# The last film of a four-layer sequence kernel: batch 0 normalized during the attention's last groups, turns and out pairs of the two batches interleaved, four stores

## What is computed

```
q = xn @ q_w + q_b;  k = xn @ k_w + k_b;  v = (xn @ v_w + v_b) * mask     # xn = layer_norm(x)
att = softmax(q k^T + mask term, over the keys)                            # 16 heads of 16 channels
y = att v                                                                  # 1024 x 256 for each batch
scale, shift = split(silu(emb) @ emb_w + emb_b)
h = layer_norm(y, sb_norm_w, sb_norm_b) * (1 + scale) + shift
return x + silu(h) @ out_w + out_b
```

## Time and profile before

| | us |
|---|---|
| median of three runs | 2120.67 |
| lowest and highest | 2118.75, 2123.79 |
| the profiled execution | 2122.75 |
| its span in the profile | 2121.0 |
| busy in the span: TensorE, VectorE, ScalarE, GpSimd | 1739.7, 1822.9, 1211.9, 1147.5 |
| mean granted TensorE clock, as a share of full speed | 0.889 |

### The profile page before, as it was taken

The page is one execution under the profiler, slowest core; times in us unless marked ns, Lnnn a source line. Parts: engine busy times, 40 slices in busy tenths (PEclk is TensorE's granted clock), DMA queues, the critical chain, the costliest instruction groups (busy, mean ns, idle before and its releaser), DMA issues.

```text
span 2121.0 us, 23810 instructions
## 1 busy us (share of the span) xinstructions
PE 1739.7 (82%) x8210; PEld 651.4 (31%) x8210; DVE 1822.9 (86%) x2159; ACT 1211.9 (57%) x2171; POOL 1147.5 (54%) x585
## 2 busy tenths in 40 slices
PE   5788879678797888678788888796897899999985
PEld 2222213132231323232322222232663333333323
DVE  4699999899999999999998999999547888888803
ACT  3766465645656666555565666543452266666672
POOL 2688877877888887789898787764000000000000
PEclk9898979869697899899997999887998799999998
DMA  6152522222223232322222232331061522220001
GB/s 198 56 160 79 95 71 75 66 61 71 75 70 98 79 95 80 87 70 72 91 81 88 74 100 73 108 90 46 1 121 39 83 33 32 32 32 2 2 2 40
DMA packets 95941, 149.83 MB, mean 71 GB/s; under 512 B 24291, under 2 KB 31651, under 8 KB 95412
## 3 DMA queue, kind: packets, MB, share of 16 engines
q1 hardware_dynamic: 95820, 148.31, 27.1%
HBM read 137.05 MB, written 10.62 MB: 70 GB/s over the span
## 4 chain that ended last, share of the span: by engine, by line
PE 40%; DVE 34%; issue 9%; POOL 8%; ACT 7%; DMA 2%; SPq 0%; DVEq 0%; ACTq 0%; POOLq 0%
DVE hbuf L2331 19%; DVE hbuf L2312 7%; PE psum L1721 6%; PE psum L731 6%; POOL hbuf L1421 6%; PE psum L697 5%; PE psum L717 4%; PE psum L612 3%; PE psum L1510 3%; DVE gain L1012 2%; PE psum L601 2%; PE psum L1673 1%; PE psum L1518 1%; PE psum L1537 1%; DMA cbuf<-scr_c 1%
## 5 line engine op out<-in xcount | busy, mean ns | idle before, releaser
L1421 POOL TENSOR_TENSOR hbuf<-hbuf,cbuf 128x1024 f32<-128x1024 f32 x384 | 901.8, 2358 | 272.9 <-DVE hbuf L2331 141.2
L2119 ACT ACTIVATE psum<-slots,cols 128x512 f32<-128x512 f32 x708 | 485.5, 689 | 392.0 <-DVE hbuf L2331 387.9
L1721 PE MATMUL psum<-hbuf,ident 64*64 64x512 f32 x3072 | 491.6, 715 | 172.8 <-POOL hbuf L1421 172.2
L2312 DVE TENSOR_TENSOR hbuf<-slots,psum 128x1024 f32<-128x1024 f32 x354 | 422.1, 1193 | 49.8 <-POOL slots L1338 30.3
L2331 DVE TENSOR_TENSOR_SCAN hbuf<-psum,hlast,hbuf 128x512 f32<-128x512 f32 x354 | 432.5, 1263 | 8.7 <-ACT psum L2119 8.7
L2331 DVE TENSOR_TENSOR_SCAN hbuf<-psum,hbuf 128x512 f32<-128x512 f32 x354 | 411.1, 1200 | 8.8 <-ACT psum L2119 8.8
L1012 DVE TENSOR_REDUCE gain<-psum 128x1 f32<-128x512 f32 x512 | 315.4, 680 | 59.2 <-PE psum L697 58.7
L563 POOL COPY wl<-hbuf 128x512 f32<-128x512 f32 x8 | 4.8, 613 | 429.1 <-PE psum L731 400.4
L697 PE MATMUL psum<-slots 99*128 99x512 bf16 x512 | 197.1, 400 | 23.9 <-DVE gain L1012 11.5
L717 PE MATMUL psum<-slots 102*128 102x512 bf16 x512 | 194.5, 388 | 6.5 <-ACT xn_flat L895 1.7
L1721 PEld LDWEIGHTS psum<-hbuf,ident 64*64 64x64 f32 x3072 | 91.0, 147 | 318.3 <-POOL hbuf L1421 255.4
(11 more groups left out here) (278 smaller groups left out, 2234.3 us busy)
## 6 DMA issues: line engine op xcount, KB each, us to landing
cbuf<-scr_c SPq DMA_DIRECT2D x384, 256.0 KB, 3.2
slots<-scr_qk SPq DMA_DIRECT2D x96, 128.0 KB
wl<-scr_diag SPq DMA_DIRECT2D x18, 256.0 KB, 4.7
scr_qk<-slots SPq DMA_DIRECT2D x8, 512.0 KB, 2.8
wl<-in_w SPq DMA_DIRECT2D x8, 496.0 KB, 4.9
wl<-in_ada_w SPq DMA_DIRECT2D x1, 3584.0 KB
xt<-in_x SPq DMA_DIRECT2D x2, 1024.0 KB, 12.5
wl<-in_w SPq DMA_DIRECT2D x2, 1024.0 KB, 7.0
```

Source lines behind the costliest of these rows:

```text
L1421: pool.tensor_tensor(hs, hs, cbuf[:, at % CRING:at % CRING + 1, :].to_broadcast([P, 2, TC]), ALU.mult).then_inc(weighed, 1)
L1721: last = pe.matmul(psum[side, bank, :], ident[rows_of, rows_of], hbuf[rows_of, at % RING, q, :], start=False, stop=n == NS - 1, skip_group ...
L2119: act.activation(decay_bank(at, q), dts[k % 2][:, e, :], ACT.Exp, scale=coefficient(WORK[k], e, n)).then_inc(decay, 1)
L2312: dve.tensor_tensor(hbuf[:, at % RING, :, :], ws[k % 2][:, 2 * p:2 * p + 2, :], psum[:, 2 + at % 2:3 + at % 2, :].to_broadcast([P, 2, TC]) ...
```

## The change

- VectorE measures and normalizes y3[0] in group 57 of the loop (MEASURE_Y3), behind that group's division; ScalarE's first `deviation()` stands behind the exps of group 58.
- The pieces of the last films are listed in another order (LAST_FILMS) and use banks 4 to 7. TensorE first makes sure that the maxima's banks have been read.
- Behind the last weighing TensorE turns batch 0 (token half 0 first: pieces 0, 2, 1, 3), then does turn_out of the last half job, then batch 0's out pairs 0 and 1 once the two silus of token half 0 are done, then batch 1's turns once y3[1] is normalized, then batch 0's pairs 2 and 3, then batch 1's four pairs, by token halves.
- ScalarE: silu table, batch 0's silus, exp table, `deviation()` for batch 1, silu table, batch 1's silus. The last load of the exp table is gone.
- VectorE: behind the last division it measures and normalizes y3[1], then adds all eight pairs.
- SP stores half a batch at a time, four DMAs of 512 KB, each as soon as its two pairs are added; `x_done` is gone.

```diff
+MEASURE_Y3 = JOBS * TT - TT + 1
...
-                  ("2hT", 1), ("2out", 1), ("3xT", 1), ("3q", 1), ("3k", 1), ("3v", 1),
-                  ("3hT", 0), ("3out", 0), ("3hT", 1), ("3out", 1)):
+                  ("2hT", 1), ("2out", 1), ("3xT", 1), ("3q", 1), ("3k", 1), ("3v", 1)):
     STAGES += [(_name, _b, i) for i in range(1 if _name == "2m" else 4)]
+BY_SIDE = (0, 2, 1, 3)
+LAST_FILMS = [("3hT", 0, i) for i in BY_SIDE] + [("3out", 0, i) for i in range(2)]
+LAST_FILMS += [("3hT", 1, i) for i in BY_SIDE] + [("3out", 0, i) for i in (2, 3)]
+LAST_FILMS += [("3out", 1, i) for i in range(4)]
+STAGES += LAST_FILMS
...
-            return psum[:, T[key] % 4, :]
+            return psum[:, T[key] % 4 + (4 if key in LAST_FILMS else 0), :]
...
+            def last_out(b, pairs):
+                to_tokens("3out", b, h3T[b], w3[:, 3], OB3, pairs)
...
             weigh(JOBS - 1, 1, TT // 2 - 1)
+            pe.wait_ge(maxed, JOBS * 2 * UNITS)
+            pe.wait_ge(max_read, JOBS)
+            pe.wait_ge(h_ready, 3)
+            to_wide("3hT", 0, y3[0], BY_SIDE)
             turn_out(2 * JOBS - 1)
-            pe.wait_ge(normalized, 2 * JOBS)
-            for b in range(BATCH):
-                film("3", 3 + b, b, y3[b], h3T[b], w3[:, 3], OB3)
+            after_act("3hT", 0, 2)
+            last_out(0, (0, 1))
+            pe.wait_ge(h_ready, 4)
+            to_wide("3hT", 1, y3[1], BY_SIDE)
+            after_act("3hT", 0, 3)
+            last_out(0, (2, 3))
+            for side in range(2):
+                after_act("3hT", 1, BY_SIDE[2 * side + 1])
+                last_out(1, (2 * side, 2 * side + 1))
...
+            def last_hidden(b):
+                for i in BY_SIDE:
+                    k, n = divmod(i, 2)
+                    act.activation(h3T[b][:, k, n * 512:n * 512 + 512], get("3hT", b, i), ACT.Silu,
+                                   scale=f_cols[:, 1, b, 0, k:k + 1], bias=f_cols[:, 1, b, 1, k:k + 1]).then_inc(t_act, 1)
...
-            for b in range(BATCH):
-                deviation()
-            for b in range(BATCH):
-                film(3, b, h3T[b])
+                if g == MEASURE_Y3 + 1:
+                    deviation()
+            act.preload_act_table_set("silu_and_others")
+            last_hidden(0)
+            act.preload_act_table_set("natural_log_exp_and_others")
+            deviation()
+            act.preload_act_table_set("silu_and_others")
+            last_hidden(1)
...
+                if g == MEASURE_Y3:
+                    dve.wait_ge(normalized, JOBS)
+                    measure(y3[0])
+                    normalize(y3[0], y3[0], h_ready)
             take_out(2 * JOBS - 1)
             divide_out(2 * JOBS - 1)
             dve.wait_ge(normalized, 2 * JOBS)
+            measure(y3[1])
+            normalize(y3[1], y3[1], h_ready)
             for b in range(BATCH):
-                measure(y3[b])
-                normalize(y3[b], y3[b], h_ready)
-            for b in range(BATCH):
-                add_out("3out", b, x_done)
+                add_out("3out", b, None)
...
             for b in range(BATCH):
-                sp.wait_ge(x_done, b + 1)
-                sp.dma_start(out[b].rearrange("(i p) d -> p i d", p=P), xt[:, b * TT:(b + 1) * TT, :]).then_inc(stored, 16)
-            sp.wait_ge(stored, 16 * BATCH)
+                for side in range(2):
+                    sp.wait_ge(t_dve, t_taken(("3out", b, 2 * side + 1)))
+                    at = b * TT + side * TB
+                    sp.dma_start(out[b, side * TC:side * TC + TC].rearrange("(i p) d -> p i d", p=P),
+                                 xt[:, at:at + TB, :]).then_inc(stored, 16)
+            sp.wait_ge(stored, 32 * BATCH)
```

More of the change, by code:

```diff
@@ L400, in build @@
         scanned, weighed, summed = sem("scanned"), sem("weighed"), sem("summed")
-        saved, y_free, x_done = sem("saved"), sem("y_free"), sem("x_done")
+        saved, y_free = sem("saved"), sem("y_free")
         ld_fcols, f_cols_ready, keep_ready = sem("ld_fcols"), sem("f_cols_ready"), sem("keep_ready")
@@ L587, in start, with to_wide @@
                 return stage_bank(key)
[L589 to L595, removed]
+            def to_wide(name, b, src, pieces=range(2 * KD)):
+                for i in pieces:
+                    ps, (k, n) = start(name, b, i), divmod(i, 2)
+                    for q in range(4):
+                        last = pe.transpose(ps[:, q * P:(q + 1) * P], src[:, n * 4 + q, k * P:(k + 1) * P], ident[:, :])
+                    last.then_inc(t_done, 1)
             def project(name, b, w, src, pieces=range(4)):
```

## The result

Seven executions of the changed kernel took 2105.09 us in the median (2097.49 to 2113.79), seven of the kernel before 2120.93 (2118.75 to 2125.02): a ratio of 0.9917, with a 95% interval of 0.9892 to 0.9941. The prediction was 2104.4. The profiled execution took 2110.42.

The account below looks back on a forecast made before the run. Engines waiting on each other in the last groups, then a serial tail, bound the kernel. TensorE's end 2100.55 + 0.11 + 0.69 + 3.39 = 2104.74 against 2121.0, 16.3 less; from median 2120.67 that gives 2104.4 us, range 2100.7 to 2110.0.

Parts of the forecast that it names:

- Term 1: Group 58 to 59: ScalarE's Ln and Exp for batch 0 add 0.54 us (bounds 0 and 1.2); VectorE's 6 us cost nothing.
- Term 2: Behind the last weighing: batch 0's turns ahead of turn_out(15) delay batch 1's measuring by 1.22 us (bounds 1.0 and 2.9).
- Term 3: Tail: batch 1's measuring starts at 2076.83 instead of 2081.65, its turns at 2083.59; all three table loads cost nothing.
- Term 4: TensorE from batch 1's turns: 1.91 us, six pairs 13.44, one low clock stretch 1.6 (bounds 0 and 4.3), ending at 2100.55.
- rival A': Tail: no fall of TensorE's clock, 1.6 us less, 2102.8 us; chance 0.15.
- Term 5: End of the kernel: 0.11 and 0.69 us for the last addition, then 3.39 for the store instead of 4.89.
- the prediction's other estimate: Last store, by the skill page's fixed 2.0 us: 3.5 us instead of 2.9, the end 0.6 later.
- Rival B: Tail: a second low stretch, from batch 0's turns through batch 1's next two pairs, 4.3 us instead of 1.6, 2107.1; chance 0.11.
- C: Tail: clock low to the end, all turns and six pairs, 13.7 us instead of 1.6, 2116.5; chance 0.04.
- D: Loop: VectorE comes late to group 57, so ScalarE stands up to 6.6 us for batch 0's normalizing, 2111; chance 0.02.
- E: Last five groups: the hole at group 59 brings the clock down, 22.8 us together, 2127, slower; chance 0.02.

Follow-up runs that it names:

- the better version: Changed kernel with batch 0's deviation behind group 58's fourth exp, turn_out between batch 0's turns, half of batch 1 normalized in the loop: 0.9899 of the kernel before.

## Why the prediction was right, point by point

- *Term 1, 0.54 for the deviation in the loop*: 0.41 by the period. VectorE had 5.35 us to spare before take_out, forecast 4.8. That nothing hides ScalarE's pair held for the place where the change puts it; behind the fourth exp it costs nothing.
- *Term 2, +1.22 for batch 0's turns ahead of turn_out*: 0.87 (3.06 against 2.19 from the copy's start to the measuring), under its lower bound of 1.0. I took the turns' 1.91 less the copy's 0.69; the turns start 0.13 before the copy, and the old turn also waited for the copy's hand-over.
- *Term 3, what falls off the chain*: from the measuring to the turns 6.73 us (2082.49 to 2089.22), forecast 6.76. The loads were hidden as said, with 1.83 us to spare for ScalarE, forecast 1.9.
- *Term 4, TensorE*: from the first turn of batch 1 to the last addition's start 15.45 us (2089.22 to 2104.67); the sum has 1.91 + 13.44 + 0.11 = 15.46 without the clock. The 1.6 us for a low stretch was not paid in the profiled execution, nor in the second one: both are rival A', to which I had given 0.15, and whose tail by the prediction's steps is 29.7. Where the stretch came, in the run with the deviation amid a group, it cost 2.7, because it held the turns and most of a pair, and I had priced it by a stretch that held pairs alone. One fall in four executions at 2.7 us is 0.7 on average, against the 1.6 of the sum. So this term was the one most in error.
- *Term 5, the store*: 3.34 from the last addition's end, forecast 3.39; four stores against two 1.6, forecast 1.5. The Trainium skill's advice to join transfers ("DMA: Bandwidth & Descriptors", "Rules for kernel authors") points the other way. For a store that ends the program the rows decide against it: 4.4, 2.9 and 2.1 us (medians) for 1024, 512 and 256 KB, by which about 1.4 is fixed and the rest goes by bytes, and only the last one's fixed part is on the path. For 512 KB that is 2.9, and not the 3.5 of the prediction's other estimate.
- *Rival B* (a low clock from batch 0's turns on) did not come: TensorE went through 20 turns in a row at the high clock. The prediction read the turns and first two pairs of the old tail as one low stretch. They were two: the clock was full from 2085.2 and fell anew in the wait of 4.38 us. Another window of the kernel before, beside the earlier trace rows:

```profile
2088.00:2089.00 1.00, 0.00 (x0) 0.00 (x0) 0.30 (x1) 1.00 (x3) 0.00 (x0) 0.79 0.00 0
```

  The Trainium skill's "TensorE: Matmul & The Clock Gate", Part 4, has transposes not counted as busy in the same way. The traces show both sides. A wait of 1.57 us behind turns was followed by a fall in three of four cases: in both executions of the kernel before and behind batch 1's turns in the run with the loop part only, but not behind batch 0's in that same run. A wait of 3.04 behind pairs brought the clock down once in four. And in the kernel before (2085.2) and in the run with all but the loop part it rose with turns alone behind it. What of this is the turns' and what is when the wait fell was not separated.
- *Rivals C, D and E* did not come: every pair took 2.24 or 2.25 us, ScalarE did not wait for the measuring in group 58, and the clock was 1.00 from 2036 to 2079.
- *The whole*: the tail came out 18.8 us shorter, 18.4 with the 0.41, against 16.3 in the sum. Of the 2.0 us by which the tail is shorter than the prediction's 31.3, 1.6 are the clock and 0.35 term 2. The medians of the spans differ by 16.0 (29 executions against 13) and their means by 17.2 with a standard error of 1.6, since each execution drifts by 4 to 5 us. So the times can't tell 16.3 from 18.4; that the mechanism held is shown by the tails. The prediction left this drift out but for the range of three runs; it is wider than that range showed, and three of the seven executions lie outside the range forecast for the median (whose upper end is 2110.2 by its own sum, not 2110.0). That the median fell within 0.7 us of the forecast is in part luck.

## What to carry to other kernels

What needs only half of the data (one batch, one half of the tokens) belongs beside the last stage that still holds the machine, at the place where its engine waits anyway: the same two activations cost 0.41 us behind a group's last exp and nothing amid a group, where ScalarE waits for the weighing. When a change moves a tail of 30 us in a kernel whose total drifts by several us, measure the tail from a mark of its own in the profile. At the end of this program only the last store is on the path, so its size is what to cut, as long as the stores before it are out of the way (256 KB landed in 2.1 us, and the next store came 2.24 later).

## What the runs showed of the hardware that was not expected

- The same program reached the same instruction 7.8 us apart in two executions (2065.09 and 2072.88), and 15 us apart for the changed one (2064.34 and 2079.43). It goes with the mean granted clock of TensorE (correlation −0.70 over 29 executions, −0.83 over 13). Where it arises, and why, was not followed.
- At one and the same wait of 3.04 us the granted clock fell in one execution and stayed in three; at a wait of 5.78 us it fell in the one execution tried. Even within one execution, the run with the loop part only, it stayed full behind one wait of 1.57 us and fell behind the next.
- A table load of 1.28 us had no further cost around it: at 2077.41 it follows the exp at once, and at 2075.31, in the better version, the Ln follows the load within 0.02 us.
